# GNN edge pass on one core: two norms' small chains and the segment marks moved between engines

## What is computed

```python
hv = layernorm(x).reshape(n, 12, 64)
ft = einsum('nhd,od->nho', hv, W)
a1 = sum(ft * attn_l, -1);  a2 = sum(ft * attn_r, -1)
e = leaky_relu(a1[src] + a2[dst], 0.2)
m = segment_max(e, dst)                      # segments: the edges of one target
w = exp(e - m[dst])
alpha = w / max(segment_sum(w, dst)[dst], 1e-16)
agg = segment_sum(alpha[:, :, None] * ft[src], dst)
x = x + relu(agg + einsum('nhd,od->nho', hv, W_res))
x = x + ffn(layernorm(x))                    # class tokens through experts, the rest gelu MLP
```

## Time and profile before

| | before |
|---|---|
| median of 3 runs | 2668.76 us (2667.09 to 2670.31) |
| the profiled execution | 2669.66 us, span 2667.8 us |
| TensorE's granted clock, mean | 0.988 of full speed |
| busy share of the span: PE, DVE, ACT, POOL | 96%, 93%, 89%, 80% |
| edge pass, about 0 to 930 us; between 400 and 600 us: PE, DVE, ACT, POOL | 97.9%, 95.5%, 90.5%, 79.4% |
| node pass, 1100 to 2600 us: PE, DVE, ACT, POOL | 99.9%, 96.3%, 94.4%, 87.6% |

### The profile page before, as it was taken

The page is one execution under the profiler, slowest core; times in us unless marked ns, Lnnn a source line. Parts: engine busy times, 40 slices in busy tenths (PEclk is TensorE's granted clock), DMA queues, the critical chain, the costliest instruction groups (busy, mean ns, idle before and its releaser), DMA issues. The chain is left out here.

```text
span 2667.8 us, 67341 instructions
## 1 busy us (share of the span) xinstructions
PE 2562.7 (96%) x20334; PEld 2315.5 (87%) x20334; DVE 2472.9 (93%) x4949; ACT 2364.0 (89%) x4748; POOL 2142.9 (80%) x2029
## 2 busy tenths in 40 slices
PE   5899999999999967999999999999999999999998
PEld 4777777777777846999999999999999999999997
DVE  6799999999999886999999999999999999999996
ACT  4999999999999955999999999999999999999993
POOL 6777777877777618888888888888888888888882
PEclk9999999999999987999999999999999999999999
DMA  8788888878888567999999999999999999999983
GB/s 313 225 268 268 266 267 264 271 265 265 265 269 266 172 210 276 353 345 336 333 333 326 323 326 324 321 319 316 310 326 316 316 318 314 313 310 311 313 311 120
DMA packets 254176, 777.85 MB, mean 292 GB/s; under 512 B 77185, under 2 KB 85165, under 8 KB 253837
## 3 DMA queue, kind: packets, MB, share of 16 engines
q1 hardware_dynamic: 184190, 563.88, 59.7%
q0 software_dynamic: 69312, 210.37, 25.5%
q10 hardware_dynamic: 432, 0.62, 0.1%
HBM read 638.86 MB, written 236.65 MB: 328 GB/s over the span
## 5 line engine op out<-in xcount | busy, mean ns | idle before, releaser
L1057 PE MATMUL ps<-wr_bd,arena 128*128 128x128 f32 x4704 | 593.9, 277 | 13.9 <-DVE arena L1457 13.9
L1057 PEld LDWEIGHTS ps<-wr_bd,arena 128*128 128x128 f32 x4704 | 563.8, 193 | 15.3 <-issue 15.2
L723 POOL DMA_INDIRECT arena<-agg_scratch,nrow x392 | 439.1, 1120 | 77.7 <-issue 66.0
L664 POOL TENSOR_SCALAR arena<-csr_neg,mv,r_n 128x768 f32<-128x768 f32 x392 | 387.2, 988 | 51.1 <-PE ps L893 37.9
L1452 DVE SCALAR_TENSOR_TENSOR ps<-ps,r_n,arena 128x768 f32<-128x768 f32 x392 | 399.1, 1018 | 12.5 <-DMA arena<-agg_scratch,nrow 10.8
L843 ACT ACTIVATE t_hi<-ps 128x768 fp32r<-128x768 f32 x392 | 314.5, 802 | 93.9 <-PE ps L893 93.8
L1457 DVE SCALAR_TENSOR_TENSOR arena<-ps,arena 128x768 f32<-128x768 f32 x392 | 375.5, 958 | 13.4
L852 ACT ACTIVATE arena<-arena,s_st 128x768 f32<-128x768 f32 x392 | 363.8, 928 | 25.0 <-DVE arena L1457 25.0
L713 POOL TENSOR_SCALAR arena<-arena,nm_n,r_n 128x768 f32<-128x768 f32 x392 | 383.2, 978 | 2.5 <-issue 1.7
L1464 DVE TENSOR_TENSOR t_lo<-ps,t_hi 128x768 fp32r<-128x768 f32 x392 | 373.6, 953 | 12.6 <-ACT t_hi L843 12.4
L811 ACT ACTIVATE arena<-arena,mv 128x768 f32<-128x768 f32 x392 | 367.8, 938 | 12.8
(11 more groups left out here) (226 smaller groups left out, 6171.5 us busy)
## 6 DMA issues: line engine op xcount, KB each, us to landing
arena<-in_x SPq DMA_DIRECT2D x196, 768.0 KB
arena<-in_x_cols SPq DMA_DIRECT2D x392, 384.0 KB, 5.2
out<-arena SPq DMA_DIRECT2D x195, 768.0 KB, 5.7
agg_scratch<-agg_ring SPq DMA_DIRECT2D x196, 384.0 KB, 3.6
dst_all<-in_dst_rows SPq DMA_DIRECT2D x28, 256.0 KB
arena<-agg_scratch,nrow POOLq DMA_INDIRECT x392
arena<-in_x,e_slot POOLq DMA_INDIRECT x364, 4.8
dst_all<-in_dst_rows SPq DMA_DIRECT2D x28, 192.0 KB
```

What stands on the lines that cost most here:

```text
L664: pool.tensor_scalar(g_ring[:, g, :].rearrange("p (c f) -> p c f", f=P), csr_neg[:, None, :].to_broadcast([P, NC, P]), mv1[:, w, 2 * (v % ...
L723: pool.indirect_dma_start(g_ring[:, g, :], None, agg_d, bass.IndirectOffsetOnAxis(nrow[:, v, 3:4], 0), bounds_check=EP - 1, oob_is_err=Fal ...
L1057: last = nc.tensor.matmul(res_ps(b, tr)[:, i * P:(i + 1) * P], xt_ring[:, g, i * P:(i + 1) * P], wr_bd[:], start=True, stop=True)
```

## The change

Three edits, all in the edge pass, for every group:

1. The source norm: POOL makes `ve_s`, the negated mean, the power and the product `nm_s` by itself (`source_scale`, four instructions where there was one). DVE's two instructions go. POOL waits for DVE's statistics (`s_ag`) and twice for its own results.
2. The target norm: POOL makes `ve_d`, the power and `nmd` (three instructions where there was one); DVE's two go. POOL waits for ACT's squares (`s_sqd`) and twice for its own results.
3. The segment marks: at chunk 12, PE transposes `same_f` once for all chunks; DVE writes marks and penalties into a piece of `agg_ring` that is not yet in use; SP writes them to memory, each row repeated for 12 heads (4 DMAs), waits until they have landed, and then loads `same_r` and `pen_r` (84x128 each) for each group, one group ahead, once the scans of the group before are over. DVE's `same_x`, `same_r` copy and `pen_r`, and PE's second transpose, go.

```diff
+        seg_d = nc.dram_tensor("seg_scratch", [2, EC, HEADS, P], f32).ap()
...
-        same_x = sb("same_x", [P, 2, HG])
...
+        seg_t = agg_ring[0:EH, 2, 0:4 * P].rearrange("p (k n e) -> p k n e", k=2, n=2)
...
+        seg_ps = ps[0:EH, 5, 2 * P:4 * P].rearrange("p (n e) -> p n e", n=2)
...
+            def load_segments(g):
+                for k, rows in enumerate((same_r, pen_r)):
+                    sp.dma_start(rows[:, 0:P], seg_d[k].rearrange("(g c) h e -> g (c h) e", c=G)[ds(g, 1)].rearrange("g r e -> (g r) e")).then_inc(d_seg, 16)
...
+                    if isinstance(b, int) and b == 1 and i == 0:
+                        sp.wait_ge(s_idx, 2)
+                        for k in range(2):
+                            for n in range(2):
+                                sp.dma_start(seg_d[k, n * EH:(n + 1) * EH], seg_t[:, k, n, :][:, None, :].to_broadcast([EH, HEADS, P])).then_inc(d_seg, 16)
+                        sp.wait_ge(d_seg, 16 * 4)
+                        load_segments(0)
+                    gs_ = 2 * b + (i - 21) // G + 1
+                    if (i - 21) % G == 0 and exists(gs_, NG) and not (isinstance(gs_, int) and gs_ < 1):
+                        sp.wait_ge(s_tot, gs_)
+                        load_segments(gs_)
...
+            def source_scale(w, gp):
+                pool.wait_ge(s_ag, G * (gp + 1))
+                at_least(pool, s_norm, G * (gp - 1))
+                settle(pool)
+                pool.tensor_scalar(ve_s[:, w, :], mvs[:, w, :, 1], EPS, None, ALU.add).then_inc(s_ve, 1)
+                pool.tensor_scalar(nm_s[:, w, :], mvs[:, w, :, 0], -1.0, None, ALU.mult).then_inc(s_ve, 1)
+                pool.wait_ge(s_ve, 2 * gp + 2)
+                settle(pool)
+                pool.tensor_tensor(r_s[:, w, :], ve_s[:, w, :], half[:, 0:G], ALU.pow).then_inc(s_rp, 1)
+                pool.wait_ge(s_rp, gp + 1)
+                settle(pool)
+                pool.tensor_tensor(nm_s[:, w, :], nm_s[:, w, :], r_s[:, w, :], ALU.mult).then_inc(s_nm, 1)
...
                     gd = 2 * b + (i - L_VD - 5) // G
                     if (i - L_VD - 5) % G == 0 and exists(gd, NG):
                         w = (i - L_VD - 5) // G % 2
+                        pool.wait_ge(s_sqd, G * (gd + 1))
+                        settle(pool)
+                        pool.tensor_scalar(ve_d[:, w, :], q_d[:, w, :], 1.0 / D, EPS, ALU.mult, ALU.add).then_inc(s_ved, 1)
                         pool.wait_ge(s_ved, gd + 1)
+                        at_least(pool, s_e, 2 * (gd - 1))
                         settle(pool)
                         pool.tensor_tensor(r_d[:, w, :], ve_d[:, w, :], half[:, 0:G], ALU.pow).then_inc(s_rpd, 1)
+                        pool.wait_ge(s_rpd, gd + 1)
+                        at_least(pool, s_eo, G * (gd - 1))
+                        settle(pool)
+                        pool.tensor_tensor(nmd[:, w, :], a2_all[:, w, :, HEADS], r_d[:, w, :], ALU.mult).then_inc(s_nmd, 1)
...
                     if isinstance(b, int) and c == G + 1:
-                        pool.wait_ge(s_ve, 1)
-                        pool.tensor_tensor(r_s[:, 0, :], ve_s[:, 0, :], half[:, 0:G], ALU.pow).then_inc(s_rp, 1)
+                        source_scale(0, 0)
                     gp = 2 * b + (i - 11) // G
                     if k == 11 % G and exists(gp, NG) and not (isinstance(gp, int) and gp == 0):
-                        w = (i - 11) // G % 2
-                        pool.wait_ge(s_ve, gp + 1)
-                        settle(pool)
-                        pool.tensor_tensor(r_s[:, w, :], ve_s[:, w, :], half[:, 0:G], ALU.pow).then_inc(s_rp, 1)
+                        source_scale((i - 11) // G % 2, gp)
...
                             act.wait_ge(d_gd[vd % G], 16 * (2 * b + (i - L_TR) // G + 1))
+                            at_least(act, s_nmd, 2 * b + (i - L_TR) // G - 1)
                             nc.scalar.activation(both_t[:, v, D:2 * D], xd_ring[:, vd, :], ACT.Copy, scale=-1.0 / D,
                                                  accum_out=a2_all[:, vd // G, vd % G, HEADS:HM]).then_inc(s_mean, 1)
...
                     if (i - 19) % G == 0 and exists(gt_, NG):
                         w = (i - 19) // G % 2
                         pe.wait_ge(s_leak, gt_ + 1)
-                        pe.wait_ge(s_dsl, gt_ + 1)
-                        nc.tensor.transpose(row_ps[:, 0:P], e_col[:, w, :], ident[:])
-                        nc.tensor.transpose(row_ps[:, P:2 * P], same_x[:, w, :], ident[:]).then_inc(s_ert, 1)
+                        nc.tensor.transpose(row_ps[:, 0:P], e_col[:, w, :], ident[:]).then_inc(s_ert, 1)
...
                     if isinstance(b, int) and c == 12:
                         pe.wait_ge(s_eqf, 1)
+                        for n in range(2):
+                            nc.tensor.transpose(seg_ps[:, n, :], same_f[:, n * EH:(n + 1) * EH], ident[:])
                         for n in range(2):
                             last = nc.tensor.matmul(cnt_ps[:, n:n + 1], eq_f[:, n * EH:(n + 1) * EH], ones[:, 0:1],
...
                     gc = 2 * b + (i - 17) // G
                     if k == 3 and exists(gc, NG):
                         w = (i - 17) // G % 2
-                        at_least(dve, s_ert, gc - 1)
                         at_least(dve, s_mask, G * (gc - 1))
                         V.tensor_copy(dst_slot[:, w, :], dstbf[:, ds(G * gc, G)])
-                        V.tensor_copy(same_x[:, w, :].rearrange("p (g h) -> p g h", h=HEADS),
-                                      same_f[:, ds(G * gc, G)][:, :, None].to_broadcast([P, G, HEADS])).then_inc(s_dsl, 1)
 
                     gv = 2 * b + (i - 7) // G
                     if k == 0 and exists(gv, NG):
-                        w = (i - 7) // G % 2
-                        dve.wait_ge(s_ag, G * (gv + 1))
-                        V.tensor_scalar(ve_s[:, w, :], mvs[:, w, :, 1], EPS, None, ALU.add).then_inc(s_ve, 1)
                         if isinstance(gv, int) and gv == 0:
...
-                    gn = 2 * b + (i - 8) // G
-                    if k == 1 and exists(gn, NG):
-                        w = (i - 8) // G % 2
-                        dve.wait_ge(s_rp, gn + 1)
-                        at_least(dve, s_norm, G * (gn - 1))
-                        V.scalar_tensor_tensor(nm_s[:, w, :], mvs[:, w, :, 0], -1.0, r_s[:, w, :],
-                                               ALU.mult, ALU.mult).then_inc(s_nm, 1)
...
                     gd = 2 * b + (i - L_VD) // G
-                    if (i - L_VD) % G == 0 and exists(gd, NG):
-                        w = (i - L_VD) // G % 2
-                        dve.wait_ge(s_sqd, G * (gd + 1))
-                        V.tensor_scalar(ve_d[:, w, :], q_d[:, w, :], 1.0 / D, EPS, ALU.mult, ALU.add).then_inc(s_ved, 1)
-
...
                         V.tensor_copy(idx_i[:], idx_f[:]).then_inc(s_idx, 1)
+                        V.tensor_copy(seg_t[:, 0], seg_ps)
+                        V.tensor_scalar(seg_t[:, 1], seg_ps, 1.0, BIG, ALU.subtract, ALU.mult).then_inc(s_idx, 1)
...
                     if exists(c, EC) and not (isinstance(c, int) and c < 2):
+                        if k == 0:
+                            at_least(dve, s_nm, 2 * b + i // G - 1)
                         source_stats(c, i, i // G, k, 2 * b + i // G)
...
@@ -1315,8 +1335,7 @@
                         dve.wait_ge(s_ert, gm + 1)
                         if exists(cf, EC):
                             at_least(dve, s_esc, on_pe(b, i - L_FT + 1))
-                        V.tensor_copy(e_row[:], row_ps[:, 0:P])
-                        V.tensor_copy(same_r[:, 0:P], row_ps[:, P:2 * P]).then_inc(s_same, 1)
+                        V.tensor_copy(e_row[:], row_ps[:, 0:P]).then_inc(s_same, 1)
...
                         dve.wait_ge(s_rpd, gd + 1)
                         dve.wait_ge(s_a2c, G * (gd + 1))
                         dve.wait_ge(s_eft, G * (gd + 1))
-                        at_least(dve, s_eo, G * (gd - 1))
-                        V.tensor_tensor(nmd[:, w, :], a2_all[:, w, :, HEADS], r_d[:, w, :], ALU.mult).then_inc(s_nmd, 1)
                         at_least(dve, s_ert, gd - 1)
                         V.tensor_tensor(e_col[:, w, :].rearrange("p (g h) -> p g h", h=HEADS), a2_all[:, w, :, 0:HEADS],
                                         r_d[:, w, :][:, :, None].to_broadcast([P, G, HEADS]), ALU.mult).then_inc(s_e, 1)
...
                     if (i - 19) % G == 0 and exists(gm, NG):
                         dve.wait_ge(s_same, gm + 1)
-                        V.tensor_scalar(pen_r[:, 0:P], same_r[:, 0:P], 1.0, BIG, ALU.subtract, ALU.mult).then_inc(s_seg, 1)
-                        dve.wait_ge(s_seg, 3 * gm + 1)
+                        dve.wait_ge(d_seg, 32 * gm + 96)
                         V.tensor_tensor_scan(f_row[:], pen_r[:, 0:P], e_row[:], -BIG, ALU.add, ALU.max)\
                             .then_inc(s_seg, 1)
-                        dve.wait_ge(s_seg, 3 * gm + 2)
```

(15 more changed lines are left out.)

## The result

The changed kernel takes **2717.27 us** (median of 4 runs, 2716.01 to 2720.05); the kernel before, beside it, 2669.53 (2667.09 to 2673.12). The ratio is 1.0179, 95% interval 1.0162 to 1.0197: slower by 48 us. The profiled execution spans 2718.1 us.

The account below looks back on a forecast made before the run. GpSimd becomes the edge pass's bound at 34.3 us per group, against 31.7 on VectorE and 32.8 before. Profiled 2669.7 + 39 for 26 groups + 3 for the marks = 2712, runs' median 0.9 lower: 2711 us, range 2645 to 2752.

Parts of the forecast that it names:

- GpSimd full, though its busy share is 79%: Edge pass before: seven chunks' transfers with gaps, 29.1 us, and powers of 2.15 and 1.58 fill GpSimd's whole 32.8 us group.
- VectorE's 1.13 us: Edge pass: instructions taken off VectorE save 1.13 us per group, from start to start; its own pace would be 31.7.
- Small operations: Norms on GpSimd: five more small adds or multiplies per group at 0.24 us each, 1.2 in all.
- the estimate that stood beside the term: Small GpSimd instructions, by the skill page: each stays near 0.1 us, the time some 18 us under the forecast.
- Waits for own results: Norms on GpSimd: four waits per group for its own results at 0.21 us each, 0.84 in all.
- Being held up: GpSimd held up by VectorE's two-input message multiply: 3.0 us per group before, 2.3 to 2.8 after, taken as 2.5.
- The sum of 34.3: GpSimd's group after the change: 29.8 + 0.84 + 1.2 + 2.5 = 34.3 us, against 32.8 before.
- Number of groups: Edge pass: 26 of 28 groups counted, without fill and drain, each 1.5 us longer: +39 us.
- The marks: Edge pass start: four writes of 2.4 MB cost 0 to 8 us once, taken as 3; later loads cost nothing.
- the signs that the prediction named: Profile after: VectorE idle 1 to 3 us for `r_d` in nearly every group, its busy share about 88%, group about 34.3 us.
- The sign against it: Edge pass: GpSimd waiting for TensorE's or VectorE's semaphores 1 us or more per group would mean it was not the bound.
- first rival: Edge pass: VectorE's saving is realised, GpSimd's small instructions costing 0.1 us and held-up time 0.7 or less; 2639 to 2650; chance 0.15.

Follow-up runs that it names:

- e3: The changed kernel with GpSimd's two powers of the edge pass replaced by a multiply, so the norms' scales are wrong numbers: 2660.3 us.
- e7: The changed kernel with the target norm as before, so the marks and the source norm's four instructions on GpSimd: 2700.7 us.
- e8: The changed kernel with the source norm as before, so the marks and the target norm's three instructions on GpSimd: 2690.7 us.
- e4: The kernel before with GpSimd's two powers of the edge pass replaced by a multiply: 2669.5 us.
- e1: The kernel before with the segment marks alone changed, both norms as they were: 2679.7 us.
- e2: The kernel before with both norms' small chains on GpSimd, the marks as they were: 2729.8 us.
- e10: The kernel before with the marks' edit alone, and GpSimd's power of the target norm one edge tile earlier in GpSimd's order: 2717.4 us.
- e6: The kernel before with VectorE's message multiply reading one tensor and a column instead of two tensors, and a running sum written beside it: 2721.2 us.
- e11: The kernel before with the marks' edit alone, and VectorE's message multiply reading one tensor and a column instead of two tensors: 2720.2 us.
- e5: The changed kernel with VectorE's message multiply reading one tensor and a column instead of two tensors, and a running sum written beside it: 2701.5 us.

## Why the prediction was right

It said 2711 us; it is 2717. The mechanism is the one named: GpSimd becomes the bound, and VectorE waits for `r_d` ahead of `e_col`. By its steps:

- **GpSimd full, though its busy share is 79%.** Right for the changed kernel: e3 takes work off GpSimd and gets most of it back, e7 and e8 add work and each pays for it. For the kernel before, the sum of 32.8 did not show it, since such a sum is always the group; e4 shows that VectorE sets the pace there, which the prediction said as well, and that GpSimd could lose 2.6 us without any gain.
- **VectorE's 1.13 us.** Its list did become shorter, but the step "a shorter VectorE list shortens the group, as long as nobody else is late" had its condition broken at once: e1 has the marks' part of the saving alone and loses 9 us. What 1.13 us less on VectorE is worth with nobody else late, no run shows.
- **Small operations.** Taken at 0.24 us each, they are 0.21 to 0.33; five make 1.28 against 1.2. So the cheap end of 0.1 is out, and the dear end of 0.37 too. With it falls the estimate that stood beside the term, from the Trainium skill (GPSIMD Engine Reference, "Elementwise — side-by-side cycle accounting"): by its 2.6 cycles per element each would have stayed near 0.1.
- **Waits for own results.** Taken at 0.21, they are 0.14 to 0.24; 0.75 a group against 0.84.
- **Being held up.** Taken at 2.5, it is 7 x (1.095 + 1.045 + 1.045 - 0.97 - 0.95 - 1.00) = 1.9: 0.6 too much. The power, held up for 0.5 before, now takes 1.52 everywhere. The 3.0 that it was taken from was a remainder, and too large: by the same reckoning the transfers of the kernel before were held up for 7 x (1.087 + 0.970 + 1.139 - 0.97 - 0.95 - 1.00) = 1.9 too, and with the power's 0.5 that is 2.4; the rest was gaps and the wait for `ve_d`.
- **Missed: the gap behind the new operations.** The next gather starts 0.69 and 0.68 us after the last small operation, where it was 0.2 after the power. The gaps sum to 87.0/253 x 21 = 7.2 us a group against 6.3, so 0.9 was left out; it makes up for what was too much in the held time. The sum of 34.3 stands against 34.4 to 34.6 in a group at full clock (34.12 as the mean over all 27), and is thus closer than its parts: that is luck.
- **Number of groups.** 27 periods grew by 1.62 us on average, 43.7, where I took 26 by 1.5. The growth is uneven: some 2 us in the middle (34.8 against 32.8), and there is none in the last two groups.
- **The marks.** The loads are never late (none of the 28 first scans waits; the one at 84.97 follows the copy at 84.65). The first group is 4.9 us later, within the 0 to 8 for the marks; but it is also 4.7 later in e2, which has no marks, and 2.9 in e1. So I had the size for only part of the reason: at the start, too, the norms on GpSimd cost time.

Of the signs that the prediction named, VectorE's busy share fell to 89.3% (178.55 of 200 us) where it said about 88, and the gathers' means stayed above 1.0. The sign against it, waits of GpSimd for TensorE of 1 us or more per group, is met by the view as it stands (14.3 us for PE in 12 groups), but 0.3 of each of these waits is the gap that is always there, and they hold hardly more. In its first rival one sum is wrong: with the dear instructions the holding that decides is 32.8 - 29.8 - 2.7 = 0.3 us, not below zero. No term of the sum rests on it.

## What to carry to other kernels

An engine that mostly starts transfers can be full at a busy share of 77%. Before giving it more work, look at what ends the gaps ahead of its instructions: a sum of durations and gaps is always the period, but gaps that are the same 0.3 us each time leave no room. Even then only taking work off it shows whether it sets the pace (e3 against e4). A step that moves from a bound engine to a "free" one is worth what the second engine's list leaves, and here VectorE's saving by the marks was worth less than nothing even before any of its work went to GpSimd (e1). On a queue with little room, an instruction placed earlier than its input is ready costs most of the wait: 1.1 of 1.45 us in e10's groups at full clock.

## What the runs showed of the hardware that was not expected

- A transfer that GpSimd starts during VectorE's message multiply with two tensors from SBUF ends 0.82 to 0.99 us after that multiply, wherever in it the start lay, up to 0.14 us before its end (163 of 163 in three kernels); with one tensor and a column it ends after its own 0.97. The order counts: the 61 transfers of the kernel before that were under way for 0.10 us or more when a multiply began took 0.95 to 1.02, and the multiply took 0.94 to 0.96 either way.
- Behind a chain of small GpSimd operations whose last one takes the power's result, the next transfer starts 0.58 to 0.69 us later; behind a power alone it is 0.20 at most, mostly 0.18 to 0.20. What makes the gap was not tried.
- VectorE halts 3.5 to 3.8 us per turn of its loop in the kernels with 5145 and 5063 VectorE instructions (e6, e11), and not in those with 4949 and 4951 (before, e5), where the same place shows 0.3 to 0.4. The halt is put down to "issue"; its cause was not tried.
